# A decoder layer with two attentions: the mask of the second one's transposed scores written into their bank by ScalarE, logits in strips, own scratch, and a new order of steps

## The reference

```python
def _L0_attn_ref(x, attn_qkvw, attn_qkvb, attn_ow, attn_ob):
    qkv = x @ attn_qkvw + attn_qkvb                     # 32 heads of 16
    scores = jnp.einsum('bhqd,bhkd->bhqk', q, k) * scale
    ctx = jnp.einsum('bhqk,bhkd->bhqd', softmax(scores), v)
    return ctx @ attn_ow + attn_ob
def _L0_xattn_ref(q, k, v, start_pos, mask):            # k = v = ctx_1024, 8 heads
    scores = jnp.einsum('bsgrd,btgd->bgrst', xq, xk) / math.sqrt(HEAD_DIM)
    probs = jax.nn.softmax(scores + mask, axis=-1)
    return jnp.einsum('bgrst,btgd->bsgrd', probs, xv)
def _L0_ffn_ref(x, weight, bias, gate_w, in_channel_scale, out_channel_scale):
    routing = jax.nn.softmax(xf @ gate_w.T, axis=1)     # 8 experts
    in_scale, out_scale = routing @ in_channel_scale, routing @ out_channel_scale
    return xf * in_scale @ sign(weight).T * out_scale + bias
x = layernorm(x + attn(x)); x = layernorm(x + xattn(x, ctx)); x = layernorm(x + ffn(x))
```

## Time and profile before

| what | value |
|---|---|
| time, median of 3 runs | 377.48 us |
| span of the profiled execution | 377.4 us |
| TensorE busy | 346.5 us (92%) |
| VectorE busy | 255.8 us (68%) |
| ScalarE busy | 157.7 us (42%) |
| POOL busy | 128.1 us (34%) |
| chain that ended last: PE, DVE, DMA | 62%, 15%, 9% of the span |

### The profile page before, as it was taken

The page is one execution under the profiler, slowest core; times in us unless marked ns, Lnnn a source line. Parts: engine busy times, 40 slices in busy tenths (PEclk is TensorE's granted clock), DMA queues, the critical chain, the costliest instruction groups (busy, mean ns, idle before and its releaser), DMA issues.

```text
span 377.4 us, 7781 instructions
## 1 busy us (share of the span) xinstructions
PE 346.5 (92%) x2840; PEld 250.4 (66%) x2840; DVE 255.8 (68%) x823; ACT 157.7 (42%) x307; POOL 128.1 (34%) x207
## 2 busy tenths in 40 slices
PE   4999988999998999999999999999899998799992
PEld 3997666798655656986667669966565575454551
DVE  0788884556886655968999548889764786752535
ACT  2748007622045675231448572214466532025430
POOL 3766520133160123452362224563111344100232
PEclk9999999999998899999999999999989999999998
DMA  7928840248763000578550104687401014600001
GB/s 265 380 75 243 206 119 4 56 136 249 173 175 96 4 12 23 138 209 244 156 170 4 36 17 126 186 241 181 116 3 36 3 52 106 181 3 4 0 2 56
DMA packets 25846, 42.33 MB, mean 112 GB/s; under 512 B 7421, under 2 KB 17801, under 8 KB 23505
## 3 DMA queue, kind: packets, MB, share of 16 engines
q1 hardware_dynamic: 25497, 41.29, 39.0%
q10 hardware_dynamic: 312, 0.55, 0.4%
HBM read 29.05 MB, written 12.32 MB: 110 GB/s over the span
## 4 chain that ended last, share of the span: by engine, by line
PE 62%; DVE 15%; DMA 9%; issue 3%; POOL 3%; SPq 3%; ACT 2%; ACTq 0%; POOLq 0%; DVEq 0%
PE bank_a L923 6%; PE bank_a L925 6%; PE bank_a L924 6%; DVE nma L741 5%; PE bank_a L1014 4%; PE bank_b L1085 4%; PE bank_a L1001 4%; PE bank_b L1074 4%; PE bank_b L1062 4%; PE bank_b L1077 3%; PE bank_b L1075 3%; SPq L350 2%; PE bank_b L1059 2%; DVE x L813 2%; DMA qs<-scr_q 2%
## 5 line engine op out<-in xcount | busy, mean ns | idle before, releaser
L629 ACT ACTIVATE pb<-bank_b 128x512 f32<-128x512 f32 x64 | 37.9, 598 | 52.4 <-PE bank_b L1077 37.3
L621 ACT ACTIVATE pa<-bank_a 128x512 f32<-128x512 f32 x64 | 36.2, 596 | 40.4 <-PE bank_a L1001 30.9
L813 DVE CUSTOM_DVE_ANT_0 x<-bank_b,mraw 128x128 bf16<-128x128 f32 x192 | 42.1, 286 | 9.5 <-PE bank_b L1062 7.1
L741 DVE TENSOR_REDUCE nma<-bank_a 128x4 f32<-128x512 f32 x64 | 39.9, 681 | 2.8 <-PE bank_a L984 2.5
L923 PE MATMUL bank_a<-xH,wH 128*128 128x256 f32 x128 | 36.4, 284 | 0.8 <-DVE wL L878 0.6
L925 PE MATMUL bank_a<-xH,wL 128*128 128x256 f32 x128 | 35.8, 279 | 0.0
L924 PE MATMUL bank_a<-xL,wH 128*128 128x256 f32 x128 | 35.7, 279 | 0.0
L1074 PE MATMUL bank_b<-idr,mH 128*128 128x512 f32 x64 | 34.6, 541 | 0.7 <-DMA qx<-mrb 0.7
L1062 PE MATMUL bank_b<-kx,qx 96*128 96x128 bf16 x256 | 23.9, 228 | 2.8 <-DMA qx<-scr_x 1.8
L1001 PE MATMUL bank_a<-qs,ks 99*128 99x128 bf16 x256 | 23.9, 232 | 1.7 <-DMA qs<-mra 0.7
L1075 PE MATMUL bank_b<-idr,mL 128*128 128x512 f32 x64 | 25.2, 394 | 0.0
(11 more groups left out here) (185 smaller groups left out, 823.5 us busy)
## 6 DMA issues: line engine op xcount, KB each, us to landing
wraw<-in_L_attn_attn_qkvw_dram SPq DMA_DIRECT2D x3, 1024.0 KB, 10.0
scr_q<-qp SPq DMA_DIRECT2D x8, 384.0 KB, 3.2
qs<-scr_q SPq DMA_DIRECT2D x8, 384.0 KB, 4.5
scr_k<-kp SPq DMA_DIRECT2D x8, 384.0 KB, 3.7
ks<-scr_k SPq DMA_DIRECT2D x8, 384.0 KB, 4.8
scr_x<-xp SPq DMA_DIRECT2D x8, 384.0 KB, 2.5
qx<-scr_x SPq DMA_DIRECT2D x8, 384.0 KB, 4.2
qs<-scr_q SPq DMA_DIRECT2D x8, 256.0 KB, 4.7
```

What stands on the lines that cost most here:

```text
L629: act.activation(pb[:, n % NPB, :], pb_bank(i, *step)[:], ACT.Exp).then_inc(*rb.is_empty(i, *step))
L741: dve.tensor_reduce(nma[:, b, 4 * j:4 * j + 4], pa_bank(i, *step)[:].rearrange("p (m t) -> p m t", m=KT), AX.X, ALU.max, negate=True).then ...
L813: last = dve.tensor_tensor_reduce(unread[:, part * P:(part + 1) * P], pb_bank(i, *step)[:, r * P:(r + 1) * P], mraw[:], -1.0, -LOWEST, ALU ...
```

## The change

- **Mask by ScalarE.** New steps `sd` stand in the table, one for each `st` of B. In an `sd` ScalarE copies the transposed mask `mT`, four times side by side, from SBUF into the bank that the `st` will have; TensorE's `st` is then the one matmul that accumulates on it. `mT` is made once, by a transpose on TensorE. The bank's bits that make a matmul accumulate must be set, so `Ring` demands that the step before in the bank filled all of it; transposes in quarters and `s` clear them with the first quarter only, and the steps that fill a bank partly (`PARTIAL`) move to the fourth bank, beside `pv`. The last group's `s` no longer has its mask from TensorE; VectorE adds it as in the other groups.
- **Logits in strips.** `rl` writes four partial sums, each in a strip of 32 columns of the array, in place of four accumulating matmuls; ScalarE copies all 128 rows, and `rt` is a matmul that adds the four and transposes.
- **Own scratch.** `qr` for `q`'s split, `xr` for x's (one half, used in turn, so VectorE's `xt` of the second sequence waits for POOL's of the first); ScalarE's wait on `b_third` ahead of `wide_b` goes. There is one copy of the stacked queries and keys, so SP now waits for the last `st` of the group before. Values stand 17 apart in place of 32.
- **x of group 1** is loaded in the first transfers, into the place of `pa`, and its transposes come before the first `s`.
- **Order.** The whole table and `UNREAD` are new (82 unread matmuls before, 76 now).

```diff
+VS = HD + 1
-MASKED = NG - 1
-UNREAD = {("C", 0, "swt", 3): 10, ("C", 0, "vb"): 11, ("A", 0, "s", 0, 0): 8, ("A", 0, "mt", 0): 6, ("A", 0, "st", 0, 0): 5,
...
+UNREAD = {('C', 0, 'vb'): 14, ('A', 0, 's', 0, 3): 2, ('A', 0, 'mt', 0): 5, ('A', 1, 's', 0, 0): 3,
+          ('A', 1, 's', 0, 3): 2, ('B', 2, 'rl', 0): 2, ('B', 2, 'rr', 1): 6, ('B', 3, 's', 0, 0): 3,
...
+PARTIAL = ("mt", "ctx", "rl", "rt", "rr")
+LAID = {"sd": "st", "sm": "s"}
...
+            if thread in threads and unit[0] in LAID:
+                k, turn = turn % 3, turn + 1
+                assert whole[k]
...
+            elif thread == "B" and unit[0] in PARTIAL:
+                k = 3
...
+        qr = sb("qr", [P, 2, H], F32)
+        xr = sb("xr", [P, H], F32)
+        x_next = at("x_next", [P, GB, H], F32, pa)
...
             load_c(0)
+            sp.dma_start(x_next[:], x[GB:2 * GB].rearrange("b p f -> p b f")).then_inc(ld_next, 16)
             sp.dma_start(oraw[:], ow.rearrange("(kt p) n -> p kt n", p=P)).then_inc(ld_ow, 16)
...
+                    if i > 0:
+                        ra.wait_emptied(sp, i - 1, "st", b, HT - 1)
                     stack(ks[:, b].rearrange("r h m t -> r h (m t)"), own(scr_k[i], b), False, k_stacked[b])
...
+                elif thread == "B" and name in LAID:
+                    of = (LAID[name], *step[1:])
+                    rb.wait_free(act, i, *of)
...
+                    held = (mT if name == "sd" else mraw)[:].rearrange("p (o t) -> p o t", o=1).broadcast_to([P, 4, P])
+                    act.activation(pb_bank(i, *of)[:].rearrange("p (r t) -> p r t", r=4), held, ACT.Copy).then_inc(*rb.is_laid(i, *of))
...
-                    act.wait_ge(b_third[u], i + 1)
                     act.activation(wide_b[:, u, :], pb_bank(i, *step)[:], ACT.Copy).then_inc(*rb.is_empty(i, *step))
...
-                    rest = wide_b[:, b]
+                    if b == 1:
+                        dve.wait_ge(b_third[0], i + 1)
+                    elif i > 0:
+                        dve.wait_ge(b_third[1], i)
+                    rest = xr[:]
...
-                    if i >= MASKED:
+                    if rb.has_mask(i, *step):
                         dve.tensor_reduce(nmb[:, b, :].rearrange("p (h k) -> p h k", k=KT)[:, 4 * (g % 2):4 * (g % 2) + 4, g // 2],
...
-                    rb.wait_free(pe, i, *step)
+                    if rb.has_mask(i, *step):
+                        rb.wait_mask(pe, i, *step)
+                    else:
+                        rb.wait_free(pe, i, *step)
...
-                    ident4 = idr[:].rearrange("p (o t) -> p o t", o=1).broadcast_to([P, 4, P])
-                    pe.matmul(d4, mH[:], ident4, start=True, stop=False)
-                    pe.matmul(d4, mL[:], ident4, start=False, stop=False)
...
-                        last = pe.matmul(dst[0:E, 0:P], gT[:, kt, :], x2T[b][:, kt, :], start=kt == 0, stop=kt == KT - 1)
+                        last = pe.matmul(dst[kt * VW:(kt + 1) * VW, 0:P], gT[:, kt, :], x2T[b][:, kt, :], start=True, stop=True)
...
-                    pe.transpose(dst[:, 0:E], lg[:, tokens(b)], idf[0:E, 0:E]).then_inc(*rb.is_full(i, *step))
+                    pe.matmul(dst[:, 0:E], lg[b][:], sum4[:], start=True, stop=True).then_inc(*rb.is_full(i, *step))
```

239 lines of the change are left out of this document (141 added, 98 removed), and 3 rows, old and new, of the table UNREAD.

## The result

The changed kernel takes 391.13 us (median of 4 runs, 388.91 to 392.88), the kernel before 376.46 us (374.02 to 378.15). The ratio is 1.037, interval 1.031 to 1.043: **slower by 3.7%**, where 351.7 us was forecast. The profiled execution of the changed kernel spans 386.9 us. TensorE has become 20.6 us less busy (346.5 to 325.9 us) and the span is 9.5 us longer.

What follows compares the result with a forecast made beforehand. TensorE was taken to bound the middle. From 377.4 us the sum took 20.6 for the middle, 3.5 for the start, 1.0 for the last group and 0.6 for the end, giving 351.7 us, own range 345 to 359.

Steps and rivals of the forecast that it cites:

- What bounds the kernel before: Middle, 75.40 to 317.87: TensorE sets the time, busy 232.6 of 242.5 us, a share of 0.96.
- The price of the pair of passes, 0.46 us: Second attention's st: dropping two mask passes saves TensorE 0.46 us each, 22.1 us for 48 in the middle.
- The price of a copy: Each st: ScalarE's mask copy of 512 columns costs 0.49 us, 23.5 us for 48 in the middle.
- At its share of 0.96: Middle: 19.8 us of TensorE work kept off, at an unchanged busy share of 0.96, gives 20.6 us of time.
- The rival of the waits: Middle: round trips over ScalarE or VectorE cut TensorE's share to 0.87; 366 us in all, chance 0.20.
- The loss of 7.4 us where VectorE is full: Middle, 180 to 190 and 260 to 270: 16 st at 0.46 us gain nothing, 7.4 us lost.
- After 352.16, -0.6 us: End, after the last group's last pv: two logits get cheaper, one of them on the chain, -0.6 us.
- The last group, -1 with bounds -3 to +7: 317.87 to 352.16: ScalarE's pace equals the old fours, two st come before the last logits, -1 us.
- The clock, a rival with 0.09 and 9 us: More TensorE pauses bring three more clock drops of 3 us each; 361 us in all, chance 0.09.
- The start, -3.5: Up to 75.40: earlier splits, loads and own scratch win half the time filled with unread matmuls, 3.5 us.
- ScalarE as the bound (387 us): Every st: mask copies come late, 13.9 us more in the middle in place of the gain; chance 0.09.
- All is kept: Middle: VectorE is never full, so the whole 28.3 us is won; 344 us, or 341; chance 0.17.

Runs made afterwards that it cites:

- before_plain: Kernel before, with VectorE taking thread B's maxima without the mask in groups 0 to 2 too: 373.86 us, ratio 0.995.
- pair_back: Changed kernel, with TensorE writing the mask of all 64 st again by two passes and ScalarE copying nothing: 401.25 us, ratio 1.062.
- fill_end: Changed kernel, with the unread matmuls of the last group and end replaced by others, in a bank nobody uses any more: 378.24 us, ratio 1.008.
- best_pair: Changed kernel with plain maxima, their transfer earlier, last group as before, last rl, rt, rr in rotating banks, all st masks by TensorE: 376.93 us, ratio 0.998.
- plain_max: fill_end, with VectorE taking thread B's maxima without the mask in all groups, one instruction in place of four: 370.46 us, ratio 0.983.
- end_rotate_again: Changed kernel, with rl, rt and rr of the last group back in the three rotating banks; a repeated run: 383.7 us, ratio 1.022.
- last_pair: Changed kernel, with TensorE writing the mask for s and st again in the last group alone, plain maxima there: 386.23 us, ratio 1.020.
- before_lay: Kernel before with its own table, ScalarE's mask copies put two tiles ahead of each st, partial steps in the fourth bank: 417.49 us, ratio 1.107.
- mrb_first: fill_end, with the transfer of B's split maxima issued ahead of two of group 1's stacks: 377.15 us, ratio 1.001.

## Why the prediction was wrong, step by step

In short: the copies were worth nearly what the sum counted for them. The sum failed where it let the new order of steps run as tight as the old one, in the middle and in the last group, and where it had no term for the bank rule, in the end.

**What bounds the kernel before: held.** TensorE set the time of the middle; 10 us off VectorE gave 1.4 us there (before_plain).

**The price of the pair of passes, 0.46 us: held from start to start, too high as TensorE's busy time.** In pair_back a step of three passes starts 0.65 us after the one before (146.25 to 146.90), for 0.69. But 48 pairs make its TensorE only 17.6 us busier than the changed kernel's in the middle (231.3 for 213.7), 0.37 each and not 0.46: a lone `st` of the changed kernel is busy 16.49 / 48 = 0.34 us, where the sum took 0.23 from passes in a row. The logits in strips are as priced: in the middle they fall from 6.24 to 2.53 us, by the 3.7 of the sum, and in fill_end the strips start at 353.81 and the next matmul at 354.17, 0.36 us later, for 0.35.

**The price of a copy: held.** Three copies in a row take 1.64 us, each 0.605, so one starts 0.52 us after the other:

```profile
334.28 1.64 ACT L683 ACTIVATE bank_b<-mT 128x512 f32<-128x512 f32 x3
```

I took 0.49 from a copy out of a bank. The Trainium skill, "ScalarE: Activation LUTs" (What ACT_TABLE_LOAD costs), gave an estimate of 0.52, and the trace agrees with it.

**"At its share of 0.96": the step that failed in the middle.** The sum counted 15.3 us for the copies and (3.7 + 1.4) / 0.96 = 5.3 for the logits and unread matmuls, and let all else of the new order stay as tight as the old. The corners give 14.0 for the copies (best_pair 11.3); that part held in the main. All the rest, the new order first of all, was to win 5.3 us and cost 11.9: that is 17.2 of the 18.5 us by which the middle missed (by the table's cuts, 240.9 for 222.4).

The same seen in TensorE: it works 0.887 of the middle (213.66 of 240.85 us). Of the 19.0 us missed by the cuts of the earlier trace rows, 10.7 are pauses (27.2 us, where the sum had 221.9 - 205.4 = 16.5) and 8.3 are busy time above 205.4: 4.5 for the pairs that were worth less, 2.0 for unread matmuls (6.43 us), and 1.8 that no run explains. The share was a property of the old table, not of TensorE: pair_back, with all the work back, has 0.908 (231.3 of 254.9). The rival of the waits had a share of 0.87, 236.1 us for the middle and 366 us in all, so the middle came out near it. What I read from the order, that the new table covers ScalarE's pairs, was right (4.4 us of waits for copies, against 23.8 in the old table). The loss of 7.4 us where VectorE is full was right in kind and too narrow in place: VectorE's maxima cost 7.8 us in the new table (plain_max). A small misreading stands in it: of the 16 tiles only 13 lie in the two stretches of the earlier trace rows, five of them in 180 to 190, so the rule itself gives 6.0 us.

**After 352.16, -0.6 us: the step that failed in the end.** The new place of the partial steps is told in the section on the change, and the sum has no term for it. It takes 7.8 us in the kernel before. In the end of the changed kernel 4.2 of the 6.3 us lost are the rule's (end_rotate_again), 1.9 more come back with other unread matmuls and a clock of 0.93 (fill_end). The price could have been read: the earlier trace rows show an unread matmul start as the logits end, and the change puts it into the bank that ScalarE has yet to empty.

**The last group, -1 with bounds -3 to +7: +7.5.** VectorE's 3.4 us more for the maxima were in the sum and taken for covered, and the new order of the steps was to win 1 us. With the mask back on TensorE (last_pair) the stage is 2.9 us shorter, and still 5.1 us longer than before's with the same mask work (38.9 for 33.8). So the larger part is the new order's, with its banks and unread matmuls. The fours, reckoned at 4.41 us, are 5.8, 7.8 and 4.4, and in fill_end 4.9, 5.4 and 4.4 at a clock of 0.91: ScalarE's 9 x 0.49 is met once in three.

**The clock, a rival with 0.09 and 9 us: it came, but is not what decided.** By the stretches TensorE was at the lower level for some 72 us (36 / 0.5), before for 12; three more stretches of 6 us were thought of. The earlier trace rows had shown one: a pause of 1.77 us, and 10 us at 0.70 behind it. The Trainium skill, "TensorE: Matmul & The Clock Gate" (Part 1), calls the low clock the default that activity releases; the trace agrees, as the stretches of 0.52 and 0.50 follow one in which TensorE was busy 6.64 of 10 us. But its price is far below (1 - clock) times the length. From the changed kernel to fill_end this product falls by 8.1 us in the last group (0.72 to 0.91), and the stage gets 1.9 us shorter. From end_rotate_again to fill_end it falls by 5.0 us in the end (0.75 to 0.93), for 1.9 us. In both the unread matmuls are others too. With the same instructions in both kernels the stretch up to `q` takes 27.44 us at 0.81 and 27.07 at 0.93.

**The start, -3.5: -2.7.** Right in size, by the first `q` of group 1 at 72.74, although the clock was 0.81 there.

**The other rivals.** ScalarE as the bound (387 us) came near the time and not the cause: the wait that it named is 4.4 us here and 23.8 in before_lay, where its cover is missing as the prediction said. "All is kept" is out. Of the prediction's signs, TensorE near 300 us busy (325.9) and a middle of 222 us failed; a clock below 0.9 in several slices came (13).

**What stays open.** Which of the other edits makes the middle of the new table 11.9 us longer with the passes in place isn't separated. pair_back's trace shows a transfer behind stacks, waits for VectorE's maxima and the clock behind these pauses, and plain maxima leave 3.8 of the 11.9; mrb_first moved the one pause and got another. What the lower clock cost by itself in the middle no run shows.

## What to carry to other kernels

Work taken from the engine that is full turns into time only as far as the next engine's results come earlier too; a busy share is a property of the order of steps, so when a change brings a new order, take the share from a stage whose order is known, and price the old work in the new order apart (two tables, two ways: four corners). Price every rule that decides which buffer a step gets, above all for steps whose job is to fill a wait: a filler that waits for a buffer is a wait itself. And where the trace before shows one drop of TensorE's clock behind one pause, count the pauses that the change makes; but don't take (1 - clock) times the length for its price, where the engine waits anyway.

## What was not expected of the hardware

TensorE's clock stayed at the lower level for 20 us (0.52 and 0.50 from 330 to 350) while TensorE was busy 7.36 and 7.88 of each 10 us, and the earlier trace rows had 10.00 of 10 at 0.70 as well: a busy engine by this count isn't a granted clock. The lower clock cost little where runs can tell: 0.4 us between 0.81 and 0.93 in the stretch up to `q`, at most 1.9 us in each of the last two, unread matmuls included. Matmuls without use, put into the pauses of the last group and the end and into a bank of their own, took 12.9 us off the kernel; 4.2 us in the end came with the banks alone. And a matmul accumulates on what ScalarE wrote into the bank, at 0.52 us a copy of 512 columns, 0.04 more than the 0.48 that the earlier trace rows show for a copy out of one.
